# Normalisation and routing work of a fused MLA attention and mixture-of-experts layer moved from VectorE to ScalarE and GpSimd

## What is computed

```python
x = _layernorm(x + attn(x))                       # x1, [8192, 256]
logits = xt @ w_router; probs = softmax(logits)
top1 = argmax(probs); gate = probs[top1]
pos = cumsum(onehot(top1), axis=0)[t, top1] - 1   # place of the token at its expert
accepted = pos < C
slot = where(accepted, top1 * C + pos, E * C)
buf = zeros((E * C + 1, H)).at[slot].set(xt)      # then the experts on buf
x = _layernorm(xt + out_tok * gate)
```

## Time and profile before

| | us |
|---|---|
| median of 3 runs | 2511.35 |
| lowest and highest | 2507.96, 2512.93 |
| profiled execution, its own time | 2510.11 |
| its span, first to last instruction | 2508.0 |
| first pair begins at | 50.9 |
| last pair begins at | 2144.1 |
| expert part, about | 2248 to 2508 |

### The profile page before, as it was taken

The page is one execution under the profiler, slowest core; times in us unless marked ns, Lnnn a source line. Parts: engine busy times, 40 slices in busy tenths (PEclk is TensorE's granted clock), DMA queues, the critical chain, the costliest instruction groups (busy, mean ns, idle before and its releaser), DMA issues.

```text
span 2508.0 us, 36804 instructions
## 1 busy us (share of the span) xinstructions
PE 2345.6 (94%) x11528; PEld 1517.6 (61%) x11528; DVE 1602.7 (64%) x4618; ACT 1015.1 (40%) x1992; POOL 1678.9 (67%) x1623
## 2 busy tenths in 40 slices
PE   6999999999999999999999999999999999949996
PEld 4555575556655665566555665566556655537774
DVE  4677657765676667765776567666776577335553
ACT  3445424443444334542444334433444344212222
POOL 1688756975787757875797568766787579623444
PEclk8999999999999999999999999999999999969998
DMA  3222100200011001100020001100110001224652
GB/s 87 60 64 81 39 14 14 73 18 14 18 49 37 18 10 39 47 18 13 18 69 18 14 18 51 35 18 9 43 43 18 18 14 55 68 79 155 193 180 68
DMA packets 96818, 118.96 MB, mean 47 GB/s; under 512 B 12289, under 2 KB 75783, under 8 KB 96625
## 3 DMA queue, kind: packets, MB, share of 16 engines
q1 hardware_dynamic: 89712, 99.98, 14.5%
q0 software_dynamic: 6912, 16.64, 1.9%
HBM read 46.91 MB, written 37.90 MB: 34 GB/s over the span
## 4 chain that ended last, share of the span: by engine, by line
PE 76%; DVE 13%; issue 6%; POOL 1%; ACT 1%; DMA 0%; DVEq 0%; SPq 0%; POOLq 0%; ACTq 0%
PE value_ps L722 18%; PE misc_ps L744 9%; PE turned_ps L699 9%; PE turned_ps L702 8%; PE misc_ps L621 8%; PE turned_ps L891 6%; PE row_ps L674 6%; PE turned_ps L674 3%; PE misc_ps L734 3%; DVE masked_row L1117 2%; DVE q_hl L1098 2%; DVE q_hl L1097 2%; DVE rinv L1151 1%; PE misc_ps L770 1%; DVE x L1199 1%
## 5 line engine op out<-in xcount | busy, mean ns | idle before, releaser
L964 ACT ACTIVATE probs<-turned_ps 128x512 f32<-128x512 f32 (+2 forms) x1280 | 652.1, 554 | 815.2 <-PE turned_ps L702 801.2
L504 POOL TENSOR_TENSOR half_sums<-half_sums,probs 128x1024 f32<-128x1024 f32 (+3 forms) x512 | 832.4, 1626 | 33.2 <-ACT probs L964 15.9
L722 PE MATMUL value_ps<-probs,lat_keys 128*64 128x512 f32 (+3 forms) x3072 | 597.7, 511 | 0.0
L699 PE MATMUL turned_ps<-q_hl,lat_hi 128*128 128x512 f32 (+2 forms) x1280 | 529.7, 414 | 1.5 <-ACT fold_v L1009 1.5
L702 PE MATMUL turned_ps<-q_max,lat_lo 65*128 65x512 f32 (+2 forms) x1280 | 483.7, 378 | 2.5 <-DMA q_max<-both_rows 2.5
L479 POOL TENSOR_SCALAR_AFFINE_SELECT probs<-probs 128x256 f32<-128x256 f32 x512 | 210.3, 411 | 405.0 <-ACT probs L964 404.1
L1117 DVE CUSTOM_DVE_ANT_0 masked_row<-row_ps,future 128x512 bf16<-128x512 f32 (+4 forms) x707 | 347.3, 511 | 189.6 <-PE row_ps L674 184.2
L499 POOL TENSOR_TENSOR half_sums<-probs 128x768 f32<-128x768 f32 (+1 forms) x128 | 269.4, 2105 | 140.8 <-ACT probs L964 118.2
L674 PE MATMUL row_ps<-lat_hi,q_hl 128*128 128x512 f32 (+4 forms) x1026 | 324.3, 356 | 33.0 <-DVE neg_max L1117 18.5
L722 PEld LDWEIGHTS value_ps<-probs,lat_keys 128*64 128x64 f32 x3072 | 190.5, 139 | 265.3 <-issue 199.8
L699 PEld LDWEIGHTS turned_ps<-q_hl,lat_hi 128*128 128x128 f32 x1280 | 244.6, 191 | 137.3 <-issue 107.9
(11 more groups left out here) (191 smaller groups left out, 2652.3 us busy)
## 6 DMA issues: line engine op xcount, KB each, us to landing
q_max<-q_hl SPq DMA_DIRECT2D x256, 128.0 KB
slots_x<-router SPq DMA_DIRECT2D x8, 1290.0 KB, 6.0
ex_x<-slots_x SPq DMA_DIRECT2D x64, 129.0 KB, 2.4
x_in<-in_L_attn_x_bld SPq DMA_DIRECT2D x8, 1024.0 KB, 5.5
layer_out<-x_in SPq DMA_DIRECT2D x8, 1024.0 KB, 4.5
ex_w<-in_L_ffn_w_gate SPq DMA_DIRECT2D x32, 256.0 KB, 3.7
ex_w<-in_L_ffn_w_up SPq DMA_DIRECT2D x32, 256.0 KB, 3.8
ex_w<-in_L_ffn_w_down SPq DMA_DIRECT2D x32, 256.0 KB, 4.3
```

What stands on the lines that cost most here:

```text
L504: nc.gpsimd.tensor_tensor(total, total, now[:, :, q0:BANK], ALU.add).then_inc(added, 1)
L699: nc.tensor.matmul(scores_of(n, h), lat_hi[b % 2][:, keys], q_hl[gp % 2][:, heads, cols], start=True, stop=False)
L722: mm = nc.tensor.matmul(value_ps[h * LD:(h + 1) * LD, q0:BANK], lat_keys[b % 2][:, j, :], probs[:, n % NPROBS, h, q0:BANK], start=(j == 0) ...
L964: nc.scalar.activation(probs[:, n % NPROBS, heads, q0:BANK], scores_of(n, h), ACT.Exp).then_inc(exp_done, 1)
```

## The change

- `normalise` in the loop goes from VectorE to ScalarE, one tile at a time (`normalise_tile`, x times rstd plus a shift), at the places of `NORMALISE_AT`: (1, 9), (1, 10), (1, 11), (2, 0), (2, 4), (2, 5) and twice (2, 6). Behind the loop it stays on VectorE.
- Epsilon, the negated mean and the shift are made in `roots` and `root` on GpSimd; `roots` stands one slot earlier, at (1, 7) and (2, 1).
- `destinations` goes to GpSimd, from (3, 11) to (4, 3), as nine instructions: eight where VectorE had seven, and the addition to `earlier`. `count` on TensorE waits for it. The DMAs of `send` move by one pair, to (5, 0) to (5, 3) and (6, 0) to (6, 3).
- `q_hl` is allocated ahead of `fold_v`.

```diff
@@ -73,2 +73,4 @@
 
+    NORMALISE_AT = [(1, 9), (1, 10), (1, 11), (2, 0), (2, 4), (2, 5), (2, 6), (2, 6)]
+
     NADD = 11
@@ -116,4 +118,4 @@
         lat_keys = [sb(f"lat_keys{i}", [P, NT, LD], F32, attn) for i in range(2)]
-        fold_v = sb("fold_v", [P, NPAIR, D], F32, attn)
         q_hl = [sb(f"q_hl{i}", [P, 2, L], F32R, attn) for i in range(2)]
+        fold_v = sb("fold_v", [P, NPAIR, D], F32, attn)
         q_max = sb("q_max", [LD + 1, 2, 2, BANK], F32R, attn)
@@ -219,2 +221,7 @@
         rstd_ready = sem("rstd_ready")
+        eps_added = sem("eps_added")
+        x1_shift_ready = sem("x1_shift_ready")
+        counted = sem("counted")
+        earlier_ready = sem("earlier_ready")
+        route_step = sem("route_step")
         x1_ready = sem("x1_ready")
@@ -516,2 +525,5 @@
                 pool.wait_ge(var_ready, b * 2 + hf + 1)
+                nc.gpsimd.tensor_scalar(var_eps[:, tiles], mean_var[:, tiles, 1], EPS, None, ALU.add).then_inc(eps_added, 1)
+                nc.gpsimd.tensor_scalar(rt[:, 9, tiles], mean_var[:, tiles, 0], -1.0, None, ALU.mult).then_inc(eps_added, 1)
+                pool.wait_ge(eps_added, 2 * (b * 2 + hf + 1))
                 nc.gpsimd.tensor_tensor(rstd[:, tiles], var_eps[:, tiles], minus_half[:, tiles], ALU.pow
@@ -519,2 +531,3 @@
                 pool.wait_ge(rstd_ready, b * 2 + hf + 1)
+                nc.gpsimd.tensor_tensor(rt[:, 6, tiles], rt[:, 9, tiles], rstd[:, tiles], ALU.mult).then_inc(x1_shift_ready, 1)
                 nc.gpsimd.tensor_tensor(alone[:, 0, tiles], rstd[:, tiles], rstd[:, tiles], ALU.mult
@@ -531,2 +544,23 @@
 
+            def destinations(b):
+
+                pool.wait_ge(counted, b + 1)
+                nc.gpsimd.tensor_scalar(rt[:, 5, :], rt[:, 3, :], float(C), None, ALU.mult).then_inc(route_step, 1)
+                nc.gpsimd.tensor_scalar(rt[:, 7, :], rt[:, 4, :], float(C), FAR, ALU.is_ge, ALU.mult).then_inc(route_step, 1)
+                pool.wait_ge(route_step, 6 * b + 1)
+                nc.gpsimd.tensor_tensor(rt[:, 5, :], rt[:, 5, :], rt[:, 4, :], ALU.add).then_inc(route_step, 1)
+                pool.wait_ge(route_step, 6 * b + 3)
+                nc.gpsimd.tensor_tensor(rt[:, 8, :], rt[:, 5, :], rt[:, 7, :], ALU.add).then_inc(route_step, 1)
+                if b:
+                    pool.wait_ge(sent, 16 * NT * b)
+                nc.gpsimd.tensor_scalar(x1[:, :, GATE], rt[:, 2, :], 0.5, None, ALU.mult).then_inc(route_step, 1)
+                nc.gpsimd.tensor_copy(x1[:, :, TOKEN].bitcast(I32), token_f[:, :]).then_inc(route_step, 1)
+                pool.wait_ge(route_step, 6 * (b + 1))
+                nc.gpsimd.tensor_scalar(token_f[:, :], token_f[:, :], float(L), None, ALU.add).then_inc(routed, 1)
+                nc.gpsimd.tensor_scalar(send_idx[:, :], rt[:, 8, :], float(SLOTS), None, ALU.add).then_inc(send_ready, 1)
+                if b < LAST:
+                    nc.gpsimd.tensor_tensor(earlier[:, :, :], earlier[:, :, :],
+                                            in_tiles[:, :].unsqueeze(1).to_broadcast([P, NT, E]), ALU.add
+                                            ).then_inc(earlier_ready, 1)
+
             def send(b, i):
@@ -552,6 +586,8 @@
                         divide(gp - 1, 1)
-                    if b and (p, t) in ((1, 8), (2, 2)):
+                    if b and (p, t) in ((1, 7), (2, 1)):
                         roots(b - 1, p - 1)
-                    if b and p in (4, 5) and t < HPB:
-                        send(b - 1, (p - 4) * HPB + t)
+                    if b and (p, t) == (4, 3):
+                        destinations(b - 1)
+                    if b and p in (5, 6) and t < HPB:
+                        send(b - 1, (p - 5) * HPB + t)
             add_probs(PAIRS - 1, NSLOT - 1)
@@ -561,2 +597,3 @@
                 roots(LAST, hf)
+            destinations(LAST)
             for i in range(NT):
@@ -571,2 +608,5 @@
                 pool.wait_ge(var_ready, 2 * B + g + 1)
+                nc.gpsimd.tensor_scalar(neg_mean[:, part], mean_var[:, part, 0], -1.0, None, ALU.mult).then_inc(eps_added, 1)
+                nc.gpsimd.tensor_scalar(var_eps[:, part], mean_var[:, part, 1], EPS / 4, None, ALU.add).then_inc(eps_added, 1)
+                pool.wait_ge(eps_added, 2 * (2 * B + g + 1))
                 nc.gpsimd.tensor_tensor(rstd[:, part], var_eps[:, part], minus_half[:, part], ALU.pow
@@ -777,2 +817,4 @@
                 pe.wait_ge(onehot_ready, b + 1)
+                if b:
+                    pe.wait_ge(earlier_ready, b)
                 nc.tensor.matmul(bank[:, 0:NT * E], before_bf[:, :], onehot[:, :, :].rearrange("p t e -> p (t e)"),
@@ -973,2 +1015,10 @@
 
+            def normalise_tile(b, i):
+
+                act.wait_ge(x1_shift_ready, b * 2 + i // HPB + 1)
+                ins = nc.scalar.activation(x1[:, i, 0:D], x1[:, i, 0:D], ACT.Identity,
+                                           bias=rt[:, 6, i:i + 1], scale=rstd[:, i:i + 1])
+                if i % HPB == HPB - 1:
+                    ins.then_inc(x1_ready, 1)
+
             def pass_alone(b, i):
@@ -1022,2 +1072,5 @@
                             STAGES[use[0]](*use[1:])
+                    for i, at in enumerate(NORMALISE_AT):
+                        if b and (p, t) == at:
+                            normalise_tile(b - 1, i)
                     if b and p == 3 and t < NT:
@@ -1187,3 +1240,2 @@
             def variance(b, hf):
-                tiles = slice(hf * HPB, (hf + 1) * HPB)
                 settle()
@@ -1191,12 +1243,11 @@
                     last = nc.vector.bn_aggr(mean_var[:, i, :], stat6[:, i, :])
-                step(last)
-                settle()
-                nc.vector.tensor_scalar(var_eps[:, tiles], mean_var[:, tiles, 1], EPS, None, ALU.add).then_inc(var_ready, 1)
+                last.then_inc(var_ready, 1)
 
-            def normalise(b, hf):
-                dve.wait_ge(rstd_ready, b * 2 + hf + 1)
-                for i in range(hf * HPB, (hf + 1) * HPB):
+            def normalise(b, tiles):
+                for i in tiles:
+                    dve.wait_ge(rstd_ready, b * 2 + i // HPB + 1)
                     last = nc.vector.tensor_scalar(x1[:, i, 0:D], x1[:, i, 0:D], mean_var[:, i, 0:1], rstd[:, i:i + 1],
                                                    ALU.subtract, ALU.mult)
-                last.then_inc(x1_ready, 1)
+                    if i % HPB == HPB - 1:
+                        last.then_inc(x1_ready, 1)
 
@@ -1241,18 +1292,4 @@
                 settle()
-                step(nc.vector.tensor_tensor(earlier[:, :, :], earlier[:, :, :],
-                                             in_tiles[:, :].unsqueeze(1).to_broadcast([P, NT, E]), ALU.add))
-                step(nc.vector.reciprocal(rt[:, 2, :], rt[:, 1, :]))
+                nc.vector.reciprocal(rt[:, 2, :], rt[:, 1, :]).then_inc(counted, 1)
 
-            def destinations(b):
-
-                settle()
-                step(nc.vector.scalar_tensor_tensor(rt[:, 5, :], rt[:, 3, :], float(C), rt[:, 4, :], ALU.mult, ALU.add))
-                step(nc.vector.tensor_scalar(rt[:, 7, :], rt[:, 4, :], float(C), FAR, ALU.is_ge, ALU.mult))
-                settle()
-                step(nc.vector.scalar_tensor_tensor(rt[:, 8, :], rt[:, 5, :], float(SLOTS), rt[:, 7, :], ALU.add, ALU.add))
-                nc.vector.tensor_scalar(x1[:, :, GATE], rt[:, 2, :], 0.5, None, ALU.mult)
-                step(nc.vector.tensor_copy(x1[:, :, TOKEN].bitcast(I32), token_f[:, :]))
-                settle()
-                nc.vector.tensor_scalar(token_f[:, :], token_f[:, :], float(L), None, ALU.add).then_inc(routed, 1)
-                nc.vector.tensor_copy(send_idx[:, :], rt[:, 8, :]).then_inc(send_ready, 1)
 
@@ -1303,8 +1340,4 @@
                         count_tiles(b - 1)
-                    if b and (p, t) == (3, 11):
-                        destinations(b - 1)
                     if b and (p, t) in ((1, 5), (2, 0)):
                         variance(b - 1, p - 1)
-                    if b and (p, t) in ((1, 10), (2, 4)):
-                        normalise(b - 1, p - 1)
             for use in ENDING:
@@ -1317,3 +1350,2 @@
                     count_tiles(LAST)
-                    destinations(LAST)
                 if use[0] == "rest" and use[2] == HPB - 1:
@@ -1321,5 +1353,5 @@
                 if use[0] == "rest" and use[2] == NT - 1:
-                    normalise(LAST, 0)
+                    normalise(LAST, range(HPB))
                     variance(LAST, 1)
-                    normalise(LAST, 1)
+                    normalise(LAST, range(HPB, NT))
 
@@ -1360,7 +1392,3 @@
                     last = nc.vector.bn_aggr(mean_var[:, g % 2 * NY + n, :], stat6[:, g % 2 * NY + n, :])
-                step(last)
-                settle()
-                nc.vector.tensor_scalar(neg_mean[:, part], mean_var[:, part, 0], -1.0, None, ALU.mult)
-                nc.vector.tensor_scalar(var_eps[:, part], mean_var[:, part, 1], EPS / 4, None, ALU.add
```

(10 more changed lines are left out.)

## The result

| | before | after |
|---|---|---|
| median of 4 runs, us | 2509.65 | 2471.06 |
| lowest and highest | 2506.58, 2512.93 | 2469.86, 2472.77 |
| span of the profiled execution | 2508.0 | 2468.2 |

The ratio is 0.9847, with a 95% interval of 0.9829 to 0.9864: 1.5% less time. The forecast was 2475 us, with a range of 2459 to 2497.

What follows compares the result with a forecast made beforehand. TensorE, busy 94%, bounds the kernel, with its waits for VectorE and the clock lost after them. Profiled 2510.1 us, less 37.5 in pairs 2 to 4, plus 1.7 given back, is 2474.3; forecast 2475 us, range 2459 to 2497.

Steps and rivals of the forecast that it cites:

- What bounds the kernel: TensorE, busy 94% of the span; other engines matter by its waits for them and the clock lost afterwards.
- The normalisation: Pair 2: VectorE's 1.97 us wait goes, 13.8 us in seven batches; a new 0.5 us wait for ScalarE comes, 3.5.
- GpSimd's shift in time: Pair 2 of batch 2: shift ready by 651.2, tile 4 due at 653.05, so ScalarE doesn't wait.
- Rival 2, the port: Shared SBUF port of VectorE and GpSimd decides, so moving counts and addresses gives nothing: 2499 us, chance 0.08.
- Token counts and addresses: Pair 3, slots 9 and 11: 1.10 off the 1.52 us wait; the 1.40 wait, in batches 2 and 3, goes.
- The clock: Half-clock pieces behind each pair 3, priced at 2.04 us, go in all seven batches once the waits go.
- The router pieces: Half-clock pieces after the router matmuls ending pair 2: 2.80 us each, kept in six of seven batches.
- The end: Moved work exposed late: 0.6 in batch 7, addresses 0.6, epsilon 0.2, tail 0.3; together +1.7 us.
- GpSimd's lateness in batch 7: Pair 6 isn't long there, so GpSimd reaches a product TensorE waits for some 0.6 us later: +0.6 once.
- Rival 4: Pair 4: nine new GpSimd instructions exceed 11.2 us, so TensorE waits; beyond 16.3 the change loses; chance 0.05.

Runs made afterwards that it cites:

- part 2: The change with VectorE normalising in the loop at (1, 10) and (2, 4) as before, roots still one slot earlier: 2464.24 us, ratio 0.9831.
- the run of the roots: The kernel before with only GpSimd's two roots one slot earlier, (1,7) and (2,1): 2481.83 us, ratio 0.9899.
- The ballast: The change with nine dependent powers of eight columns added on GpSimd behind the addresses at (4, 3): 2556.19 us, ratio 1.0183.
- part 1 alone: The change with token counts and addresses back on VectorE at (3, 9) and (3, 11), sends in pairs 4 and 5: 2493.29 us, ratio 0.9945.

## Why the prediction came out right

*What bounds the kernel.* Right: all that was won lies in TensorE's waits in pairs 2 to 4 and in the clock behind them. Pairs 0 and 1 stayed at 37.26 and 44.65 us, but for batch 7's pair 1 (45.00).

*The normalisation.* The size was right: 1.97 gone, 0.40 new (0.5 predicted, though its own times, 661.44 - 660.83, give 0.6), ScalarE's tile at 600 ns by the median (589 taken), GpSimd's shift in time. The reason was half right, so this term came out by luck. The prediction saw that the long ones of VectorE's instructions fall where GpSimd works, and then costed only their removal. It counted the move of the roots as a matter of the shift's due time. The runs show that this move alone ends the meeting; once it is made, the removal to ScalarE gains nothing and, at the places of the change, costs 0.40 us a batch and some clock. The change is 5 to 7 us slower than its own part 2. What each step is worth, in us less than the kernel before on the same chip:

| | counts, addresses on VectorE | on GpSimd, with epsilon (part 2) |
|---|---|---|
| roots as before | 0 | 13.8 |
| roots one slot earlier | 24.9 | 43.6 |
| the same, ScalarE normalises (epsilon on GpSimd in both) | 14.5 | 38.6 |

ScalarE's normalisation with the roots where they were was not run, so what the removal would be worth by itself stays open. Nor was it tried whether a slot's shift would also shorten the addition of the token counts. It takes 1.16 us in the loop and 0.42 behind it, where GpSimd is idle:

```profile
L1242 DVE TENSOR_TENSOR earlier<-earlier,in_tiles x8: 425/1162/1169, 437.5 to 2229.5; 128x256 bf16<-128x256 bf16 x8
```

*Rival 2, the port.* It was set up so that part 2 gives nothing. Part 2 alone gave 43.6 us. But the meeting with GpSimd's sums was the cause of the largest wait, and moving work in time on GpSimd was the cheaper cure. The Trainium skill (SBUF — State Buffer, SBUF: two separate sides) calls the pair of SBUF ports that VectorE's two-port modes and GpSimd share an exclusive lock: whoever starts first has it for the whole instruction, and the other blocks. The trace agrees in its times: 1.34 us for four without a sum beside them, 3.86 and 4.65 with, and both of these end 0.15 us behind the end of a sum. Which mode VectorE ran in, no run shows.

*Token counts and addresses.* Slot 9's wait fell from 1.52 to 0.44, 1.08 where 1.10 was taken. The 1.40 is gone, and it would have stood in more batches than two once their clock was good, as the run of the roots shows (five). The matmuls of "pos" never wait for the new semaphore.

*The clock.* The late pieces went in all seven batches, as said, and pair 4 fell by the 2.04 taken for them. As the price of a clock piece that is too much: 1.5 and 1.6 by the two runs that show it apart; the rest was VectorE's addresses, which left in the same change. The router pieces are what the sum had too dear: six at 2.80 = 16.8 us. There are five of 3.4 us at half clock, in pair 3, and two of 6.8. Part 2 alone has a batch with no piece, with pair 3 at 28.94. So the five cost 30.00 - 28.94 = 1.1 each, and the two, with pairs 2 and 3 at 33.94 and 31.10 against 33.47 and 28.94, 2.6 each: 10.6. So all seven batches have a piece, where the kernel before had none in batch 2, but shorter ones in five. The difference of 6.2 is nearly all that parts -44.1 from the predicted -37.5. Without a piece the stretch is 33.47 + 28.94 + 27.41 = 89.82; 89.87 was predicted. Why the router pieces are shorter was not tested.

*The end.* +1.7 predicted, +3.6 measured. The term that was too small is GpSimd's lateness in batch 7: 0.6 predicted; measured 1.07 of new wait and 0.62 more in the old. The addresses cost 1.1 more (0.6 predicted): 0.08 stands ahead of nearly every instruction, not ahead of three. The epsilon costs 0.4, less 0.17 that VectorE saves (0.2 predicted), the tail 0.4 (0.3). This miss and that of the router pieces have opposite signs, which is luck too: the forecast is 4 us off, the loop alone 6.6.

*Rival 4.* Not reached: the small instructions took 0.20 to 0.27 us. The ballast showed its arithmetic to be short by almost half: it puts the loss at 15.4 + 2.9 - 11.2 = 7.1 us a batch, about TensorE's wait (6.7) without the clock after it.

## What to carry to other kernels

When a short VectorE instruction takes several times its least duration, look at what GpSimd runs at that moment, and try to move the one or the other by a slot before moving work to another engine. Undo a change part by part: a step that was moved only so that the rest fits can hold most of the gain. A long wait in a busy stream of matmuls should be priced with the half-clock piece that may follow it: here the waits of 1.5 to 2.8 us had one behind them in many batches, at about 1.5 us where two runs show its price apart, and those of 0.4 to 0.7 in pairs 2 and 3 none right behind them.

## What was unexpected of the hardware

- The half-clock piece doesn't follow from the length of the wait alone. With the 1.69 us wait at the end of pair 3 it came in seven of seven batches, with 1.52 in seven of seven of part 1 alone, but with the same 1.52 in only four of seven where nothing but the roots had moved; batch 2 has none there although a wait of 1.39 follows. After the 1.97 in pair 2 of the kernel before it came in two, after the 2.76 in seven. What else decides is open; it was not tried apart.
- A power of eight columns took 1.63 us on GpSimd in the ballast and 1.04 on four columns in the roots, while a multiply of the same eight took 0.25.
- Normalising with a step of two cost VectorE nothing (four in 3.85 us against 3.86) and gained nothing against GpSimd.
